# First-half output turned by DMA transposes, chunk products two channels sooner, sizes on ScalarE, another order at the end

## The reference

```
K[h, l]  = 2 Re sum_n Cs[h, n] exp(dtA[h, n] l),   dtA = (-exp(log_A_real) + i A_imag) dt
y[b, h]  = (causal convolution of x[b, h] masked with K[h] + x D[h]) masked again
w[k, n]  = q[k, n] s[g, n] - (z[g, n] + 1) s[g, n],  g = k // 128
gate, up = y2 @ Wg, y2 @ Wu          # y2: [2048, 1024], Wg and Wu: [1024, 2752]
out      = x + float16((gate * sigmoid(gate) * up) @ Wd)
```

## Time and profile before

| | us |
|---|---|
| median of 3 runs | 1173.37 (1173.34 to 1173.43) |
| profiled execution, its own time | 1176.32 |
| its span | 1174.4 |
| TensorE busy with matmuls | 1149.5 (98%) |
| VectorE busy | 887.7 (76%) |
| ScalarE busy | 847.5 (72%) |
| GpSimd busy | 222.0 (19%) |
| mean of one `take_down` (L1023) | 1.283 |
| mean of one shift (L959) | 0.749 |
| mean of one copy of a down scale and gate (L703) | 0.665 |

### The profile page before, as it was taken

The page is one execution under the profiler, slowest core; times in us unless marked ns, Lnnn a source line. Parts: engine busy times, 40 slices in busy tenths (PEclk is TensorE's granted clock), DMA queues, the critical chain, the costliest instruction groups (busy, mean ns, idle before and its releaser), DMA issues.

```text
span 1174.4 us, 15087 instructions
## 1 busy us (share of the span) xinstructions
PE 1149.5 (98%) x5562; PEld 954.5 (81%) x5562; DVE 887.7 (76%) x985; ACT 847.5 (72%) x1398; POOL 222.0 (19%) x139
## 2 busy tenths in 40 slices
PE   5999999999999999999999999999999999999996
PEld 5999998788888888888888888888888888888883
DVE  7678745677777777777777988887777777777775
ACT  6443204887888788788788797777888887888873
POOL 0122000211422422211111252111211211211213
PEclk8999999999999999999999999999999999999999
DMA  7878778441653556434434875455344334444514
GB/s 282 283 229 254 238 263 222 111 108 27 159 138 99 150 147 178 109 87 121 115 81 118 261 186 143 152 180 160 91 108 120 96 108 111 105 108 108 152 53 163
DMA packets 66976, 173.94 MB, mean 148 GB/s; under 512 B 11654, under 2 KB 17222, under 8 KB 66902
## 3 DMA queue, kind: packets, MB, share of 16 engines
q1 hardware_dynamic: 64834, 171.14, 50.7%
q10 hardware_dynamic: 2036, 1.81, 0.5%
q0 software_dynamic: 32, 0.03, 0.0%
HBM read 159.94 MB, written 15.83 MB: 150 GB/s over the span
## 4 chain that ended last, share of the span: by engine, by line
PE 94%; DMA 2%; DVE 2%; issue 1%; POOL 0%; ACT 0%; SPq 0%; DVEq 0%; POOLq 0%
PE pair L1257 28%; PE pair L1298 27%; PE pair L1278 27%; PE pair L1211 11%; DMA toep<-kernel_padded 1%; PE pair L1170 1%; PE pair L1191 0%; DMA kernel_padded<-k_sb 0%; POOL o L590 0%; PE pair L1327 0%; PE pair L1360 0%; DMA logs<-in_L_cond_log_dt_dram 0%; PE pair L1347 0%; PE pair L1338 0%; DVEq L175 0%
## 5 line engine op out<-in xcount | busy, mean ns | idle before, releaser
L1023 DVE SCALAR_TENSOR_TENSOR acc<-pair,s_down,acc 128x1024 f32<-128x1024 f32 x328 | 420.3, 1283 | 189.7 <-PE pair L1298 189.3
L703 ACT ACTIVATE pair<-pair,ratio 128x512 f32<-128x512 f32 x616 | 382.3, 665 | 101.4 <-PE pair L1257 101.2
L722 ACT ACTIVATE pair<-pair,ratio 128x512 f32<-128x512 f32 x581 | 360.7, 659 | 117.8 <-PE pair L1278 117.7
L1257 PE MATMUL pair<-high,wg 128*128 128x512 f32 x704 | 278.6, 396 | 0.0
L1257 PE MATMUL pair<-low,wg 128*128 128x512 f32 x704 | 277.1, 394 | 0.0
L1298 PE MATMUL pair<-mid_h,wd 128*128 128x512 f32 x688 | 268.2, 392 | 0.0
L1298 PE MATMUL pair<-mid_l,wd 128*128 128x512 f32 x672 | 265.7, 395 | 0.0
L1278 PE MATMUL pair<-high,wu 128*128 128x512 f32 x672 | 265.0, 394 | 0.0
L1278 PE MATMUL pair<-low,wu 128*128 128x512 f32 x672 | 264.0, 393 | 0.0
L542 POOL CAST mid_h<-sil 128x1024 fp32r<-128x1024 f32 (+1 forms) x43 | 45.2, 1052 | 694.5 <-DVE sil L1000 684.0
L1257 PEld LDWEIGHTS pair<-high,wg 128*128 128x128 f32 x704 | 132.1, 188 | 31.3 <-ACT pair L703 1.1
(11 more groups left out here) (150 smaller groups left out, 589.9 us busy)
## 6 DMA issues: line engine op xcount, KB each, us to landing
q_in<-rows_backwards SPq DMA_DIRECT2D x86, 512.0 KB, 4.6
z_in<-zeros_plus_one SPq DMA_DIRECT2D x130, 256.0 KB, 4.7
toep<-kernel_padded SPq DMA_DIRECT2D x64, 512.0 KB, 6.7
q_in<-_L_ffn_down_qweight_dram SPq DMA_DIRECT2D x42, 512.0 KB, 4.8
u_all<-in_x_dram SPq DMA_DIRECT2D x13, 512.0 KB, 10.9
x_fin<-in_x_dram SPq DMA_DIRECT2D x12, 512.0 KB, 9.3
out_dram<-x_fin SPq DMA_DIRECT2D x12, 512.0 KB, 5.6
high_parts<-staged SPq DMA_DIRECT2D x8, 512.0 KB, 2.9
```

Source lines behind the costliest of these rows:

```text
L703: act.activation(gate_ps[:, tb, :], gate_ps[:, tb, :], ACT.Copy, scale=ratio[:, 0, G * t + g:G * t + g + 1]).then_inc(gate_scaled, 1)
L722: act.activation(up_ps(tau)[:, tb, :], up_ps(tau)[:, tb, :], ACT.Copy, scale=ratio[:, 1, G * t + g:G * t + g + 1]).then_inc(up_scaled, 1)
L1023: dve.scalar_tensor_tensor(out=acc[:, hid, :], in0=ps, scalar=scale, in1=acc[:, hid, :], op0=ALU.mult, op1=ALU.add).then_inc(down_taken, 1)
L1257: mm = pe.matmul(gate_ps[:, tb, :], w["g"][tau % 2][:, g, :], rows[:, g, 512 * tb:512 * tb + 512], start=g == 0 and part == 0, stop=part = ...
```

## The change

The diff does the following.

- Head: chunks 0 and 1 get their sizes from eight ScalarE exponentials with a scale per partition (`first_sizes`), in place of a VectorE product and one exponential; the first angles are read from PSUM; the copies of the turned input stand in another order, and the second half of turn 5 on TensorE stands behind `multiply_kernel(0)`.
- Convolutions: `multiply_kernel` of chunks 3 to 8 stands ahead of the second channel (`hh == 1`) in place of the fourth. In iteration 12 of SP's loop the Toeplitz loads stand ahead of the first two weight loads.
- Output of the first half: `turn_out` is gone. SP issues 32 DMA transposes (128 partitions by 256 columns of float16) from `o16` into the new tile `turned`, four in each of tiles 25 to 32, and stores and loads `x` between them. `finish` is eight single steps, at g = 1 and 3 of tiles 26, 28, 30 and 32, and reads `turned`.
- End: token tiles 0 and 1 alone are summed on TensorE, their `rows_first` behind units 3 and 7, `rows_second` behind unit 11. Tiles 2 to 7 are turned and added on VectorE. SP stores the tiles in order.

```diff
...
@@ -111,24 +111,14 @@
...
+def down_at(tau, hid):
+    return NH * tau + hid
...
     return tau if is_tail(tau) else tau + 1
-def turns_before(n):
-    return sum(TURN_AT + TURN_STEP * j < n for j in range(4))
-def down_at(tau, hid):
-    n = NH * tau + hid
-    return n + turns_before(n)
-def turn_at(j):
-    return TURN_AT + TURN_STEP * j + 1 + j
...
@@ -258,6 +248,7 @@
...
         staged = sb("staged", [P, HALF], F32R)
+        turned = sb("turned", [P, 2, HID], F16)
...
@@ -325,7 +317,7 @@
...
         def last_turn_ps(tt):
-            return down_ps[tt // 2 % 2][:, tt % 2, :].bitcast(F16)
+            return down_ps[(tt // 2 - 1) % 2][:, tt % 2, :].bitcast(F16)
@@ -439,6 +431,7 @@
...
                     store_kernels(chunk_begun_at(g - 2))
+                load_toeplitz(g + 2)
@@ -446,7 +439,6 @@
...
                     load_weights("u", 0)
-                load_toeplitz(g + 2)
@@ -462,6 +454,24 @@
...
                 sp.dma_start(dst, x_slot(hf, tt)).then_inc(out_stored[tt % 4], 16)
+            def turn_and_store(v):
+                j, part = divmod(v, 2)
+                if v == 0:
+                    sp.wait_ge(o16_done, NH)
+                elif part == 0:
+                    sp.wait_ge(out_ready, 2 * j)
+                    for tt in (2 * j - 2, 2 * j - 1):
+                        store_out(0, tt)
+                if j < 4:
+                    for hid in range(4 * part, 4 * part + 4):
+                        sp.dma_start_transpose(turned[:, :, P * hid:P * hid + P], o16[:, hid, 2 * P * j:2 * P * j + 2 * P]
+                                               ).then_inc(rows_turned, 16)
+                if part and j in (1, 2):
+                    for tt in (2 * j + 2, 2 * j + 3):
+                        sp.wait_ge(out_stored[tt % 4], 16)
+                        load_x(0, tt)
@@ -485,16 +495,8 @@
...
                         load_x(0, tt)
-                if NT + 3 <= tau < NT + 7:
-                    for tt in range(2 * (tau - NT - 3), 2 * (tau - NT - 3) + 2):
-                        if tt % 2 == 0:
-                            sp.wait_ge(out_ready, tt // 2 + 1)
-                        else:
-                            sp.wait_ge(down_taken, turn_at(tt // 2) + 1)
-                        store_out(0, tt)
-                        if 2 <= tt < 6:
-                            sp.wait_ge(out_stored[tt - 2], 16)
-                            load_x(0, tt + 2)
+                if TURN_FROM <= tau <= TURN_FROM + HALF_G:
+                    turn_and_store(tau - TURN_FROM)
@@ -503,11 +505,11 @@
...
                 load_x(1, tt)
-            for tt in (0, 1, 4, 5, 2, 6, 3, 7):
-                if tt < 4:
+            for tt in range(HALF_G):
+                if tt < 2:
...
                 else:
-                    sp.wait_ge(last_added, tt - 3)
+                    sp.wait_ge(last_added, tt - 1)
@@ -624,25 +626,31 @@
...
             act.wait_ge(ident_in_sb, 16)
-            act.activation(warm[:], ident[:, 0:1], ACT.Sin)
+            act.activation(warm[:, 0:1], ident[:, 0:1], ACT.Sin)
...
                 act.copy(par_h[:, 1, n, :], aim[:]).then_inc(par_ready, 1)
+            take_rows(0, 1)
...
             act.activation(cs[:], arg_c[:], ACT.Sin, bias=tab[0:H, C_NHPI:C_NHPI + 1]).then_inc(first_done, 1)
-            take_rows(0, 3)
-            sizes(1, 0, 8)
-            act.activation(warm[:], ident[:, 0:1], ACT.Sin)
-            take_rows(3, 4)
+            take_rows(1, 3)
+            act.activation(warm[:, 1:2], ident[:, 0:1], ACT.Exp)
+            act.wait_ge(par_copied, 1)
+            for h in range(8):
+                act.activation(size[:, h, :], tab[:, C_B:C_B + 64], ACT.Exp, scale=par[:, 0, h:h + 1]
+                               ).then_inc(first_sizes, 1)
+            act.activation(warm[:, 0:1], ident[:, 0:1], ACT.Sin)
+            take_turned(3, 0)
             angles(0)
+            take_turned(3, 1)
...
             take_rows(8, HEAD_TURNS)
-            sizes(2, *place_of(2))
+            sizes(1, *place_of(2))
...
@@ -756,8 +764,6 @@
...
                     copy_sum(1)
-            for tt in (2, 3):
-                copy_sum(tt)
@@ -844,8 +850,12 @@
...
             dve.tensor_tensor(par_h[:, 3, 1, :], p3[:], p4[:], ALU.subtract).then_inc(par_ready, 1)
+            dve.wait_ge(tab_in, 16)
             dve.wait_ge(par_turned, 1)
-            do(dve.tensor_copy(par[:], par_ps[:, 0:4 * H].rearrange("p (v h) -> p v h", v=4)))
+            dve.tensor_copy(par[:, 0], par_ps[:, 0:H]).then_inc(par_copied, 1)
+            theta_0 = bass.AP(par_ps.tensor, par_ps.offset + H, [par_ps.ap[0], [1, 4], [0, 64]])
+            do(dve.tensor_tensor(theta[:, 0:4], theta_0, bass.AP(tab[:].tensor, C_B, [[C_N, P], [0, 4], [1, 64]]), ALU.mult))
+            dve.tensor_copy(par[:, 1:4], par_ps[:, H:4 * H].rearrange("p (v h) -> p v h", v=3)).then_inc(par_copied, 1)
@@ -888,7 +898,10 @@
...
                 a, b = arg[:, here, 32:64], cosine[:, here]
-                dve.wait_ge(sizes_done, max(c, 1))
+                if c < 2:
+                    dve.wait_ge(first_sizes, 4 * c + 4)
+                else:
+                    dve.wait_ge(sizes_done, c - 1)
@@ -1042,26 +1055,20 @@
...
-                dve.wait_ge(last_turned, tt - 3)
-                dve.wait_ge(x_fin_in[tt], 16)
+                dve.wait_ge(last_turned, tt - 1)
+                dve.wait_ge(x_fin_in[tt], 48 if tt < 4 else 16)
...
-            def finish(j):
-                at = turn_at(j)
-                dve.wait_ge(down_mm, at + 1)
-                for i in range(2):
-                    tt = 2 * j + i
-                    dve.wait_ge(x_fin_in[tt % 4], 16 * (tt // 4 + 1))
-                    to = x_slot(0, tt)
-                    dve.tensor_tensor(to, down_ps[at % 2][:, i, :].bitcast(F16), to, ALU.add
-                                      ).then_inc(out_ready if i == 0 else down_taken, 1)
-            dve.wait_ge(tab_in, 16)
-            exp_sizes(0, 0, 8)
-            turn_angles(0)
+            def finish(tt):
+                dve.wait_ge(rows_turned, 16 * NH * (tt // 2 + 1))
+                dve.wait_ge(x_fin_in[tt % 4], 16 * (tt // 4 + 1))
+                to = x_slot(0, tt)
+                dve.tensor_tensor(to, turned[:, tt % 2], to, ALU.add).then_inc(out_ready, 1)
             reduce_angles(0)
+            dve.wait_ge(par_copied, 2)
@@ -1115,8 +1122,8 @@
...
                         center("d", TAIL)
-                    if TURN_AT <= n < TURN_AT + 4 * TURN_STEP and (n - TURN_AT) % TURN_STEP == 0:
-                        finish((n - TURN_AT) // TURN_STEP)
+                    if g in (1, 3) and tau > TURN_FROM and (tau - TURN_FROM) % 2 and tau < TURN_FROM + HALF_G:
+                        finish(tau - TURN_FROM - 1 + g // 2)
@@ -1152,17 +1159,17 @@
...
                     take_last(e)
-            for tt in range(4, HALF_G):
+            for tt in range(2, HALF_G):
...
-            def turn(g):
+            def turn(g, halves=(0, 1)):
...
                 pe.wait_ge(x_loaded[g], 16)
-                for k in range(2):
+                for k in halves:
@@ -1178,8 +1185,9 @@
...
             mm.then_inc(par_turned, 1)
-            for g in range(3, 6):
+            for g in range(3, 5):
                 turn(g)
+            turn(5, (0,))
@@ -1197,7 +1205,7 @@
...
                         multiply_kernel(2)
-                    if hh == 3 and chunk_begun_at(g - 2) is not None:
+                    if hh == 1 and chunk_begun_at(g - 2) is not None:
@@ -1226,6 +1234,7 @@
...
             multiply_kernel(0)
+            turn(5, (1,))
@@ -1318,10 +1327,7 @@
...
-                if tt < 2:
-                    pe.wait_ge(down_taken, down_at(LAST - 1, NH - 2 + tt) + 1)
-                else:
-                    pe.wait_ge(sum_copied, 2 * (tt - 1))
+                pe.wait_ge(down_taken, down_at(LAST - 1, NH - 2 + tt) + 1)
@@ -1334,6 +1340,8 @@
...
                 taken_before(NH)
+                if tt == 0:
+                    pe.wait_ge(ident16_ready, 1)
@@ -1342,24 +1350,12 @@
...
-                taken_before(2 * NH)
+                taken_before(2 * NH if tt >= 4 else 11 + tt)
+                if tt >= 6:
+                    pe.wait_ge(last_added, tt - 5)
...
                 mm.then_inc(last_turned, 1)
-            def turn_out(j):
-                at = turn_at(j)
-                if j == 0:
-                    pe.wait_ge(o16_done, NH)
-                    pe.wait_ge(ident16_ready, 1)
-                pe.wait_ge(down_taken, at - 1)
-                for i in range(2):
-                    to = down_ps[at % 2][:, i, :].bitcast(F16)
-                    for hid in range(NH):
-                        mm = pe.transpose(to[:, P * hid:P * hid + P],
-                                          o16[:, hid, P * (2 * j + i):P * (2 * j + i) + P], ident16[:])
-                mm.then_inc(down_mm, 1)
@@ -1372,32 +1368,19 @@
...
                             down(n // NH, n % NH)
```

(41 more changed lines are left out.)

## The result

| | before | after |
|---|---|---|
| median of 6 runs on one chip, us | 1173.4 | 1185.65 (1185.14 to 1186.08) |
| ratio, with its 95% interval | | 1.0095 (1.0077 to 1.0112) |
| profiled execution, its own time and its span | 1176.32, 1174.4 | 1186.08, 1183.9 |
| mean granted clock of TensorE | 0.995 | 0.987 |

The change makes the kernel slower by 0.95%, about 12 us by the medians and 9.5 us by the profiled spans. The forecast was 1181.9 us.

The account below looks back on a forecast made before the run. TensorE's timeline was taken as the clock. Waits +12.5, clock +4.1, Toeplitz loads -2.0, head 0, transposes -3.5 and end -2.6 gave +8.5 on the median of 1173.37: 1181.9 us, range 1172 to 1187.

Parts of the forecast that it names:

- Bound: Whole kernel: TensorE holds 94% of the last-ending chain, so its idle time and work taken from it count at full size.
- Waits on chunk products: Convolutions: products of chunks 3 to 8, two channels sooner, make TensorE wait for `combine` on VectorE, +12.5 us.
- Clock: Behind the new waits in the convolutions: two to three short falls to 1.2 GHz, 2.4 x 1.7 = +4.1 us.
- Rival 1: After the new waits the clock never falls: +4.4, 1177.8 us; chance 0.24.
- Toeplitz loads: Before convolution 14: TensorE's wait goes, with loads ahead of weights and chunk 8's product sooner, -2.0 us.
- Head: Start of the kernel: 0.6 us gained before the first product, 0.86 given back by half a turn; put at 0.
- Transposes: First half's output: 64 TensorE transposes go, -3.5 us; DMA transposes stay hidden, 8 us at most for four.
- Rival 2: First half's output: DMA transposes take over some 3.2 us each, VectorE then TensorE wait, 1193.9 us; chance 0.06.
- End: Last sums and stores: six VectorE additions back to back -1.8, stores queuing less -0.8, together -2.6 us.
- Rival 3: Convolutions: sooner products let VectorE get ahead, all six waits and the falls go: -8.1, 1165.3 us; chance 0.12.
- Rival 4: No change: the two collisions with GpSimd fall elsewhere and the clock holds, +0.3, 1173.7 us; chance 0.08.

Follow-up runs that it names:

- Filling the waits: Changed kernel with 10, 7 and 8 unread matmuls on TensorE ahead of the products of chunks 5, 6 and 7: 1179.22 us, ratio 1.0042.
- the third channel: Changed kernel with the products of chunks 3 to 8 ahead of the third channel in place of the second: 1172.08 us, ratio 0.9979.
- the fourth channel again: Changed kernel with the chunk products back ahead of the fourth channel, measured once more with more rounds: 1166.39 us, ratio 0.9925.

## Why the prediction was right, and where its sizes were off

- **Bound.** Reading TensorE's timeline as the clock was right. In the trace the waits that were put there delay the first gate product at full size, and the transposes taken away are gained at full size behind it.
- **Waits on chunk products.** Forecast 4.4, 3.0, 3.6, 0.9, 0.4 and 0.1, measured 4.30, 2.87, 3.45, 0.84, 0.32 and none: 11.8 for 12.5. The method holds to 0.15 us a chunk: the new slot is the old start less two channels, the readiness is the old end of `combine`, and the waits before move both alike. The collisions with GpSimd came again: L910 takes 2.44 us in chunks 5 and 6. It ends 0.27 us behind GpSimd's subtraction (97.46 + 2.54 = 100.00). By the Trainium skill, page SBUF — State Buffer, section SBUF: two separate sides, a VectorE operation with two SBUF inputs and a GpSimd one that reads SBUF exclude each other for a whole instruction. This trace agrees in the main: L910 takes 0.42 us where no subtraction runs beside it, and here it ends 0.27 after the subtraction.
- **Clock.** The step that was mis-sized. Forecast 2.4 falls of 1.7 us, 4.1; measured three falls of 2.1, 3.0 and 1.7, 6.8. I had priced the fall by the shorter of the two stretches in the head, and the count was short by 0.6 of a fall. Filling the waits showed the cause, and the third channel showed that 2 us of waiting can be enough. Rival 1, the clock never falls, is refuted.
- **Toeplitz loads.** Forecast -2.0; in the change the whole 2.0 us wait is gone, and the loads moved alone gave 1.7 by the trace. But the term has two causes: the product at the second channel alone also removed the wait, so in the change the new load order added nothing that can be seen. It counts where the products stand at the fourth channel.
- **Head.** Forecast 0. Convolution 0 starts at 29.96 in place of 29.89. Right, as far as it can be told: chunk 1's product starts at 29.2 to 29.6 in the six traces with the old head and at 29.2 to 30.2 in the seven with the new.
- **Transposes.** Forecast -3.5, measured -3.55. VectorE reaches the first addition 11.4 us after the group of four starts, as worked out. A transpose takes 1.25 us of SP's queue and has landed 3.1 us (median) after its issue, so four are there in 3 x 1.3 + 3.1, about 7 us; with the slowest landing, 5.7, it is 9.6, so my 8 at most was too tight, but still under the 11.4. Rival 2 needed over 3.2 us for each and is refuted. Of the two pages, VectorE: DVE Perf Modes, section The three transpose paths, of the Trainium skill, has 1309 ns for a block; these DMAs of two blocks follow each other every 1.25 to 1.3 us, about half of that a block, and the measurement decides. Advanced Engine Details and Errata, section X-Bar Transpose (TRN2), of the same, has them as fast as plain DMAs: the 2.3 us of the fastest landing beside 2.0 for the plain 64 KB one nearly agrees, the median of 3.1 less so, and the issue on SP, 1.25 us beside 0.59 for a weight load, is dearer.
- **End.** The additions were forecast at -1.8 and measured at -1.8. The stores behind them: the mechanism came (1.1 us apart), the size was -2.0 instead of -0.8. Alone it gave -0.6, and with the waits filled the same end as the changed kernel's gave -0.6 too, so what this term is worth differs by 1.4 us from one trace to another; why isn't settled.
- **Rivals 3 and 4.** Rival 3 (VectorE gets ahead) was wrong: `combine` ended later than before, not sooner. The run with `combine` first shows that it names a real lever, which the diff didn't pull. Rival 4 needed the collisions to fall elsewhere, and they didn't.
- **From the sum to the median.** The sum was +8.5, the spans give +9.5. That the sum came so near is in part luck: the clock was 2.7 us dearer than forecast, and the end, 1.2 better, and the waits, 0.7 shorter, took most of it back. The other 2.7 us of the miss lie in the last step. I carried over that the profiled execution of before was 2.95 above its median, but that of the changed kernel was only 0.4 above its own. The two periods of the second half explain such a difference: the profile of before had 22.19, its second trace 21.97, and its single times spread from 1170.7 to 1179.5, while the changed kernel's all lie within 1 us. Whether the change itself sets the period I can't tell: 21.97 was seen in one trace of the kernel before and in that of the version with the waits filled, 22.18 or 22.19 in all others.

## What to carry to other kernels

Before moving an operation on the bounding engine forward, work out when its input is ready and from what that time counts: if it is a point in the producer's queue, a slot earlier than that point buys nothing and only adds a wait, so move the producer in its queue first (here one line separated 12 us lost from 8.8 us won). Price a wait on TensorE of some 3 us or more, between full work, with 1.4 to 3.0 us more of low clock, and count on it as possible from 1.7 us: of the eight waits between 1.57 and 2.02 us here, three brought a fall. Take transposes off a full TensorE by DMA where the consumer comes later than number x 1.3 us plus one landing, 2.3 to 5.7 us here.

## What the runs showed of the hardware

- **A wait of about 2 us is on the edge of a clock fall.** From convolution 0 to the first gate product, falls came behind waits of 1.74 (twice), 2.02 and all six from 2.85 to 4.31 us, and none behind 1.57 and 1.96 (the kernel before), 1.65 (the end alone), 1.65 (the fourth channel again) and 2.01 (the waits filled). The wait before convolution 14 went either way. What decides it no run here separates.
- **A fall costs 1.4 to 3.0 us** (nine of them, by the distance of products or the time of 128 matmuls).
- **Two periods in each half**, at the same granted clock: in the second half 22.19 us a tile or 21.97 (one trace of the kernel before and the one with the waits filled), in the first 22.29 or 22.24 (the fourth channel twice, the second channel alone, and the waits filled). They don't go together. The cause stays open.
